# Causal attention on one Trainium2 core: even and odd query tiles on the two column halves of the array, weights summed on GpSimd, sums inverted through DRAM

## What is computed

```python
q = (x @ w_q) ...; k = (x @ w_k) ...              # 8 heads of 64
gates = sigmoid(x @ w_gate); sel = argmax(gates)  # 8 experts a head
gm = one_hot(sel) * gates
values = einsum('bhne,ehdk,bnd->bhnk', gm, value_experts, x)
sim = einsum('bhid,bhjd->bhij', q * SCALE, k)
sim = where(causal_mask, finfo.min, sim)
attn = softmax(sim, axis=-1)
out = einsum('bhij,bhjk->bhik', attn, values)
out = einsum('bhne,ehkd,bhnk->bhnd', gm, output_experts, out).sum(axis=1)
```

## Time and profile before

| | us |
|---|---|
| median of 3 runs | 974.07 |
| profiled execution, its own time | 970.34 |
| its span, first to last instruction | 968.6 |
| TensorE busy | 931.0 |
| VectorE busy | 680.5 |
| ScalarE busy | 389.7 |
| GpSimd busy | 239.3 |
| mean granted TensorE clock | 0.996 of full speed |

### The profile page before, as it was taken

One profiled execution on the slowest core, in us unless ns is written; L12 is line 12 of the kernel. 1 busy time (PEld: TensorE's weight loads), 2 busy tenths in 40 slices (PEclk: granted clock), 3 DMA queues, 4 the chain that ended last, 5 costly groups with the idle time before them and its releaser, 6 DMA issues.

```text
span 968.6 us, 14634 instructions
## 1 busy us (share of the span) xinstructions
PE 931.0 (96%) x5580; PEld 721.1 (74%) x5580; DVE 680.5 (70%) x1054; ACT 389.7 (40%) x678; POOL 239.3 (25%) x253
## 2 busy tenths in 40 slices
PE   6989899999999999999999998999999999999998
PEld 3568678887666655899966786888876656569998
DVE  4858566547557877898868666754674777879887
ACT  4635555030566766401034355720115655751000
POOL 6212322222533322146610032300041101411000
PEclk9999999999999999999999999999999999999999
DMA  7112000524245511255630000022220000023663
GB/s 258 50 37 96 1 1 8 170 91 131 66 154 194 198 43 44 65 176 175 190 115 1 1 1 1 1 94 87 86 82 7 23 22 1 25 75 101 194 181 124
DMA packets 33739, 81.56 MB, mean 84 GB/s; under 512 B 5847, under 2 KB 10551, under 8 KB 33671
## 3 DMA queue, kind: packets, MB, share of 16 engines
q1 hardware_dynamic: 32391, 76.44, 24.9%
q10 hardware_dynamic: 1280, 4.20, 1.6%
HBM read 61.26 MB, written 19.20 MB: 83 GB/s over the span
## 4 chain that ended last, share of the span: by engine, by line
PE 81%; DVE 11%; issue 3%; ACT 3%; DMA 1%; ACTq 0%; POOL 0%; SPq 0%; DVEq 0%; POOLq 0%
PE ps L1109 18%; PE ps L1436 10%; PE ps L1373 9%; PE ps L1442 5%; PE ps L1333 5%; PE ps L1288 5%; PE ps L1117 4%; PE ps L1349 4%; PE ps L1240 3%; DVE region L1001 3%; PE ps L1302 3%; PE ps L1409 3%; PE ps L1410 2%; PE ps L1255 2%; PE ps L1151 2%
## 5 line engine op out<-in xcount | busy, mean ns | idle before, releaser
L1373 PE MATMUL ps<-region 128*128 128x512 f32 (+3 forms) x384 | 161.4, 503 | 0.0
L980 DVE TENSOR_REDUCE region<-ps 128x1 f32<-128x512 f32 (+1 forms) x192 | 98.1, 550 | 63.9 <-PE ps L1352 63.8
L761 ACT ACTIVATE region<-ps 128x512 f32<-128x512 f32 x192 | 92.3, 487 | 122.6 <-PE ps L1412 110.8
L1025 DVE COPY_PREDICATED region<-region,ps 128x512 f32<-128x512 uint32 x112 | 82.0, 735 | 72.1 <-PE ps L1109 71.4
L1436 PE MATMUL ps<-expert_hi,kst 128*128 128x256 f32 x512 | 125.1, 283 | 3.0 <-DVE kst L1055 2.2
L1436 PE MATMUL ps<-expert_lo,kst 128*128 128x256 f32 x512 | 123.3, 279 | 0.0
L1109 PE MATMUL ps<-expert_hi,wide_hi 128*128 128x512 f32 x256 | 102.7, 401 | 0.0
L551 ACT ACTIVATE region<-ps 64x512 f32<-64x512 f32 (+4 forms) x148 | 82.1, 557 | 48.3 <-PE ps L1255 21.2
L1109 PE MATMUL ps<-expert_hi,wide_lo 128*128 128x512 f32 x256 | 100.1, 391 | 0.0
L1109 PE MATMUL ps<-expert_lo,wide_hi 128*128 128x512 f32 x256 | 99.8, 390 | 0.0
L1436 PEld LDWEIGHTS ps<-expert_hi,kst 128*128 128x128 f32 x512 | 96.3, 188 | 4.2 <-DVE kst L1055 2.6
(11 more groups left out here) (151 smaller groups left out, 1764.1 us busy)
## 6 DMA issues: line engine op xcount, KB each, us to landing
region<-hot_rows SPq DMA_DIRECT2D x128, 128.0 KB, 3.3
expert_hi<-halves_kept SPq DMA_DIRECT2D x24, 512.0 KB, 3.6
expert_lo<-halves_kept SPq DMA_DIRECT2D x24, 512.0 KB, 5.1
halves_kept<-expert_hi SPq DMA_DIRECT2D x16, 512.0 KB, 5.2
halves_kept<-expert_lo SPq DMA_DIRECT2D x16, 512.0 KB, 5.9
expert<-in_value_experts SPq DMA_DIRECT2D x8, 512.0 KB, 4.2
expert<-in_output_experts SPq DMA_DIRECT2D x8, 512.0 KB, 4.3
gb<-gate_rows ACTq DMA_DIRECT2D x16, 256.0 KB, 3.9
```

What stands on the lines that cost most here:

```text
L761: act.activation(PT[:, g % RING, lo:CH], ps[:, 4 + g % 2, 0:CH - lo], ACT.Exp).then_inc(sem["pt_ready"], 1)
L980: dve.tensor_reduce(mx[:, i, at_mx:at_mx + 1], ps[:, max_bank(h, m), 0:w], AX.X, ALU.max).then_inc(sem["s_max"], 1)
L1025: dve.copy_predicated(V3_heads[:, t], chosen.unsqueeze(3).broadcast_to([P, PAIRS3, 2, HD3]), ps[:, n % 4, :].rearrange("p (a i k) -> p a i ...
L1373: mm(ps[:, SUM_BANK[c], lo:CH], V3[:, j, h // 2, h % 2 * HD3:(h % 2 + 2) * HD3], PT[:, g % RING, lo:CH], start=(j == 0), stop=(j == TC * ( ...
```

## The change

- A block is now ordered by key tile, then chunk. The exps of one key tile for all its queries are kept whole, in places that stand free (`kept`: xT, the old PT space and the x of the other batch element, whose load moves behind the first attention).
- `weigh(h, j)` does one key tile: two products with 64 stationary columns (values only), the even query tiles into PSUM partitions 0 to 63 and the odd ones into 64 to 127 of one bank. It is called behind block 6 (tiles 0, 1), block 9 (2, 3) and block 1 of the next head (4 to 7).
- GpSimd adds the weights of key tiles 1 to 7 into those of tile 0 (`add_weights`), and `denominators(h)` sums them over the partitions with two products against ones, behind block 6 of the next head; for the last head behind output step 1.
- For the first three pairs the sums go to DRAM and come back as 128 rows of 16, VectorE inverts them and multiplies by the gates (`factors`), they go to DRAM again and are broadcast into `gb`, and one multiplication per part is left. The last pair is inverted in its full form.
- The second half of `qq` and `kx` are made by DMAs on ScalarE's queue instead of copies.
- `project` stands behind `scores` in its block; the places of rounding, of pieces and of the last normalisations move.

```diff
     G = H3 * E3
-    BLOCKS = [(c, j) for c in range(NC) for j in range(TC * (c + 1))]
+    BLOCKS = [(j, c) for j in range(TT) for c in range(j // TC, NC)]
     NB = len(BLOCKS)
+    LAST_BLOCK = [max(n for n, (x, _) in enumerate(BLOCKS) if x == j) for j in range(TT)]
...
+        den_cols = hg_all[:, BY_COLUMNS * KN:(BY_COLUMNS + 2) * KN].rearrange("p (i k) -> p i k", i=2)
+        sets = lambda v: v.rearrange("p (u s c) -> p u s c", s=2, c=P)
+
+        def total(h):
+
+            return xT[:, h % 2, :]
+
+            if j == 0:
+                return total(h)
+            home = PT_all if j in (1, 2, 5) else X[:, 1 - b].rearrange("p t d -> p (t d)")
+            return home[:, KEPT_AT[j]:KEPT_AT[j] + (TT - j) * P]
...
+        ROUND_AT = {(5, 4): 0, (5, 6): 1, (6, 4): 2, (6, 6): 3, (7, 9): 4, (7, 11): 5}
-        NORMALISED_AFTER = (0, 1, 4)
+        NORMALISED_AFTER = (1, 2, 4)
...
-        SUM_BANK = (3, 7)
+        SUM_BANK = (7, 3)
+        LATE_AT, SUMS_AT, EARLY_AT, MIDDLE_AT = 1, 6, 6, 9
+        OUT_AT, DEN_AT = 3, 8
...
-            sp.dma_start(X[:, 1, :, :], xv[1]).then_inc(x_next, 16)
...
+            def keep_den(b, h):
+
+                until(sp, "den_sb", b, den_copies(h))
+                sp.dma_start(den_rows[b, h].rearrange("(u s c) -> s u c", s=2, c=P),
+                             rden[0:P:HALF, h % 2 * CH:(h % 2 + 1) * CH].rearrange("s (u c) -> s u c", c=P)
+                             ).then_inc(den_kept, 16)
+            def turn_den(b, p):
+
+                n = b * BY_COLUMNS + p
+                sp.wait_ge(den_kept, 32 * (n + 1))
+                if n >= 2:
+                    sp.wait_ge(factors_kept, 16 * (n - 1))
+                sp.dma_start(den_cols[:, p % 2, :], columns_of(den_rows[b, 2 * p:2 * p + 2])).then_inc(den_in, 16)
+            def spread_factors(b, p):
+
+                n = b * BY_COLUMNS + p
+                until(sp, "factors_ready", b, p + 1)
+                sp.dma_start(columns_of(factor_rows[b, 2 * p:2 * p + 2]), den_cols[:, p % 2, :]
+                             ).then_inc(factors_kept, 16)
+                sp.wait_ge(factors_kept, 16 * (n + 1))
+                until(sp, "oT_ready", b, NC * p)
+                for i in range(2):
+                    sp.dma_start(gb[i * HALF:(i + 1) * HALF, :],
+                                 factor_rows[b, 2 * p + i:2 * p + i + 1, :].broadcast_to([HALF, S])
+                                 ).then_inc(gates_in, 16)
...
+                if b + 1 < B:
+                    until(sp, "av_used", b, H3 * TT)
+                    until(sp, "summed", b, H3 * (TT - 1))
+                    sp.dma_start(X[:, b + 1, :, :], xv[b + 1]).then_inc(x_next, 16)
...
+                def add_weights(h, j):
+
+                    done = h * (TT - 1) + j - 1
+                    if j == 1:
+                        until(pool, "av_used", b, h * TT + 1)
+                    until(pool, "pt_ready", b, h * NB + LAST_BLOCK[j] + 1)
+                    part = total(h)[:, j * P:]
+                    pool.tensor_tensor(part, part, kept(b, h, j), ALU.add).then_inc(sem["summed"], 1)
+                    until(pool, "summed", b, done + 1)
+                        if n in LAST_BLOCK[1:]:
+                            add_weights(h, LAST_BLOCK.index(n))
...
+                def queries_twice(h):
 
                     i, own, oth = h % 2, HALF * (h % 2), HALF * (1 - h % 2)
-                    if k == 0:
-                        until(act, "qk_sb", b, (h // 2 + 1) * 2 * NC)
-                        if h >= 2:
-                            until(act, "st_ps", b, (h - 1) * NB)
-                        copy(qq[i][own:own + HALF, :], raw[own:own + HALF, 0, :], "qq_ready")
-                    elif k == 1:
-                        copy(qq[i][oth:oth + HALF, :], raw[own:own + HALF, 0, :], "qq_ready")
-                    else:
-                        copy(kx[i][own:own + HALF, :], raw[own:own + HALF, 1, :], "kx_ready")
+                    until(act, "qq_ready", b, h + 1)
+                    act.dma_start(qq[i][oth:oth + HALF, :].bitcast(fp32), qq[i][own:own + HALF, :].bitcast(fp32)
+                                  ).then_inc(qq_in, 16)
+
+                def keys_twice(h):
+
+                    i, own = h % 2, HALF * (h % 2)
+                    until(act, "kst_ready", b, 2 * h + 1)
+                    act.dma_start(kx[i][own:own + HALF, :].bitcast(fp32), kst[i][own:own + HALF, :].bitcast(fp32)
+                                  ).then_inc(kx_in, 16)
 
...
                     act.wait_ge(rows_kept, 32 * (b + 1))
-                    until(act, "oT_ready", b, NC * p)
+                    until(act, "den_ps", b, H3 - 1)
+                    until(act, "oT_ready", b, NC * (p - 1) + 1)
...
+                def output_copy(h, s):
+
+                    own, r = HALF * (h % 2), slice(s * HALF, (s + 1) * HALF)
+                    until(act, "av_used", b, (h + 1) * TT)
+                    copy(sets(oT[own:own + HALF, h // 2, :])[:, :, s, :],
+                         ps[r, SUM_BANK[h % 2], :].rearrange("p (u c) -> p u c", c=P), "o_sb")
+
+                def den_copy(h):
+
+                    own, den = HALF * (h % 2), ps[:, SUM_BANK[h % 2], :]
+                    until(act, "den_ps", b, h + 1)
+                    if h < 2 * BY_COLUMNS:
+                        n = 2 * BY_COLUMNS * b + h - 1
+                        if n > 0:
+                            act.wait_ge(den_kept, 16 * n)
+                        copy(rden[:, h % 2 * CH:(h % 2 + 1) * CH], den, "den_sb")
+                    else:
+                        act.wait_ge(den_kept, 32 * BY_COLUMNS * (b + 1))
+                        for s in range(2):
+                            copy(sets(rden[own:own + HALF, :])[:, :, s, :],
+                                 den[s * HALF:(s + 1) * HALF].rearrange("p (u c) -> p u c", c=P), "den_sb")
...
+                        if j == 0 and h >= 2:
+                            until(act, "den_ps", b, h - 1)
+                        if j and h:
+                            until(act, "av_used", b, (h - 1) * TT + j + 1)
+                            until(act, "summed", b, (h - 1) * (TT - 1) + j)
+                        act.activation(kept(b, h, j)[:, q0 - j * P:q1 - j * P], ps[:, 4 + g % 2, 0:q1 - q0], ACT.Exp
+                        if h + 1 < H3 and n == 0:
+                            queries_high(h + 1)
+                        if h + 1 < H3 and n == 1:
+                            queries_twice(h + 1)
+                        if h + 1 < H3 and n == 2:
+                            keys_twice(h + 1)
+                        if h and n in (OUT_AT, OUT_AT + 1):
+                            output_copy(h - 1, n - OUT_AT)
+                        if h and n == DEN_AT:
+                            den_copy(h - 1)
+                        if (h, n) == (H3 - 1, MIDDLE_AT):
+                            spread_gates()
                         if (h, n) in ROUND_AT:
                             rounded(ROUND_AT[h, n])
...
+                def factors(p):
+
+                    n = b * BY_COLUMNS + p
+                    if p == 0:
+                        dve.wait_ge(gate_cols_in, 16 * BY_COLUMNS * (b + 1))
+                    dve.wait_ge(den_in, 16 * (n + 1))
+                    step(dve.reciprocal(den_cols[:, p % 2, :], den_cols[:, p % 2, :]))
+                    dve.tensor_tensor(den_cols[:, p % 2, :], den_cols[:, p % 2, :], gate_cols[:, p, :], ALU.mult
+                                      ).then_inc(sem["factors_ready"], 1)
+                    if p >= BY_COLUMNS:
+                        step(dve.tensor_tensor(rden[:, cs], rden[:, cs], factors_of(p)[:, cs], ALU.mult))
+                    until(dve, "o_sb", b, 2 * (2 * p + 2))
+                    dve.tensor_tensor(oT[:, p, cs], oT[:, p, cs], (gb if p < BY_COLUMNS else rden)[:, cs], ALU.mult
...
+                    _, c0, c1 = PARTS[k]
+                    until(dve, "den_sb", b, den_copies(H3 - 1))
+                    step(dve.reciprocal(rden[:, c0:c1], rden[:, c0:c1]))
...
+                    if h >= 4 and h % 2 == 0:
+                        factors(h // 2 - 2)
+                    if h >= 4 and h % 2 == 0:
+                        weighted(h - 4)
+                        weighted(h - 3)
+                factors(BY_COLUMNS - 1)
+                weighted(H3 - 4)
+                weighted(H3 - 3)
...
-                        until(pe, "qq_ready", b, 2 * h + 2)
+                        pe.wait_ge(qq_in, 16 * (b * H3 + h + 1))
...
+                def weigh(h, j):
-                    mm(ps[:, SUM_BANK[c], lo:CH], V3[:, j, h // 2, h % 2 * HD3:(h % 2 + 2) * HD3],
-                       PT[:, g % RING, lo:CH], start=(j == 0), stop=(j == TC * (c + 1) - 1)
-                       ).then_inc(sem["av_used"], 1)
+                        if j == 0:
+                            until(pe, "val_v", b, TT * (E3 - 1))
+                    if j == 0 and h >= 2:
+                        until(pe, "den_sb", b, den_copies(h - 2))
```

(34 more changed lines are left out.)

170 lines of the change are left out of this document (86 added, 84 removed).

## The result

The changed kernel takes 1031.1 us (median of 4 runs, 1028.8 to 1032.9) against 974.2 us: a ratio of 1.0586, with a 95% interval of 1.0557 to 1.0616. The profiled execution takes 1030.4 us with a span of 1028.6, 60.1 us more than the one of before. Forecast were 1024 us and slower with 0.84.

The account below looks back on a forecast made before the run. TensorE was taken as the bound (96% busy, 81% of the chain). Profiled 970.3 us plus 9.9 and 12.7 (heads), 22.4 (last head), 2.0 (DRAM), 3.4 (clock) made 1020.7, as a median 1024 us; range 988 to 1050.

Parts of the forecast that it names:

- the forecast's sign: Weighted sums on TensorE, one of the signs that would show the forecast right: busy for 60% of the earlier time.
- The transfer's latency and issue: Second query half by DMA: issued at 3.4 us, 3.6 or 4.0 to land; scores start at 7.0 instead of 4.08.
- The wait for the row of maxima: In heads without a projection, only score block 9 covers the reduction after the last score: 0.6 us of waiting.
- The clock in the heads: TensorE's waits of about 3 us in the heads: no clock loss counted, 24 us as the other end.
- rival (c): The clock also falls in the heads, 24 us more: 1048 us; chance 0.2.
- trip through DRAM: Heads 4 and 5's sums via DRAM: 1 us waiting per batch element, 2 in all; other end 8.
- Behind the last head: Head 7's denominators and division in the output loop: 11.2 us per batch element, 22.4 in all, plus 3.4 for clock.
- What TensorE saves: Paired column halves run together in the weighted sums: 2.6 us saved in a head, 41 in sixteen heads.
- (a): Faster: scores not late, so the heads give back 35 us while the end costs 22; 961 us; chance 0.11.
- (b): Heads lose as forecast, but the division behind the last head is covered or lands earlier: 999 us; chance 0.12.
- (d): The column halves do not overlap with real operand sizes, 4.3 us in 16 heads: 1093 us; chance 0.02.
- (e): GpSimd's additions at twice their time make the denominators hold TensorE, about 1.5 us a head: 1048 us; chance 0.07.

Follow-up runs that it names:

- experiment 1: The changed kernel with the queries' second half made by ScalarE's copy again instead of the DMA: 998.1 us, ratio 1.0272.
- experiment 4: The changed kernel without the last pair's reciprocals and their multiplication by the gates (heads 6 and 7 not normalised): 1013.6 us, ratio 1.0438.
- experiment 2: The changed kernel with unread filling products on TensorE, six before each head's wait for queries and thirty before the output steps' wait: 1023.4 us, ratio 1.0525.
- experiment 9: The changed kernel with GpSimd's additions in head 7 from key tile 4 on cut to one column: 1024.9 us, ratio 1.0537.
- experiment 3: The changed kernel without the odd query tiles' products for key tiles 1 to 6: 1035.4 us, ratio 1.065.
- experiment 8: On top of experiments 7, ScalarE copies the queries' own half before the first exp instead of behind it: 984.0 us, ratio 1.0110.
- experiments 7: On experiment 1 plus earlier last-head denominators: row of maxima behind the second weighted sums, pair weightings behind the key splitting: 988.6 us, ratio 1.0154.

## Why the forecast was right, and where it wasn't

**Slower, by the forecast mechanisms: right.** The first scores are late by a transfer into qq in all 14 heads, one wait of over 7 us stands in each batch element's output steps, the reciprocals of 256 columns are gone from the heads. Taking the transfer away gives back 33 us (experiment 1), the last division 17.5 (experiment 4). The weighted sums with their ones-products are busy for 93.7 us instead of 161.4, 58% where the forecast's sign was 60%.

**The transfer's latency and issue: mis-sized, too large in quiet heads, too small in loaded ones.** The sum took 3.6 and 4.0 us from the nearest transfer; measured are 2.9 (the median of 16) and up to 6.2. That one reads DRAM, this one moves within SBUF. The Trainium skill ("DMA: Bandwidth & Descriptors", Anatomy of one DMA) has 2.0 us fixed, for transfers from GpSimd's queue, while this one is ScalarE's; the estimate of 2.6 that the forecast set beside its own is nearer to the 2.9 than the row was. The issue was put behind the exp at 3.4 us, and it came at 2.5. So a quiet odd head (3 or 5) lost 0.4 us and not 1.9, which is what 5.45 instead of 7.0 us makes of the forecast's own formula (1.9 - 1.55 = 0.35). Head 4 of the first batch element lost 6.4. Head 0, for which the sum had 0.3, lost 1.6 and, in the second batch element, 3.9: its transfer took 4.5 us there, TensorE waited 3.19 us, and two periods at the lower clock followed.

**The wait for the row of maxima: nearly right.** 0.6 us were forecast in heads without a projection; it is 0.5 us in all 14, those with a projection too; in the program the projection's products stand behind the row of maxima.

**The clock in the heads: the step that failed.** The forecast took nothing for the waits in the heads, with 24 us as the other end and 0.2 for rival (c), because TensorE is fully busy before and after. The mean granted clock fell from 0.996 to 0.972: over the spans, 1028.6 x 0.028 less 968.6 x 0.004 is 24.9 us of full clock withheld. There are 15 more periods of 3.4 us at the lower level than in before, eleven in the heads and four behind the 7.3 us waits. In the heads they cost up to 11 x 1.7 = 19 us. What this looks like in the changed kernel, first around the wait of 3.19 us that ends at 764.16, then behind the one of 1.57 us that ends at 806.31:

```profile
763.10:769.90 6.80, 5.74 (x18) 4.47 (x19) 1.49 (x4) 0.94 (x2) 0.00 (x0) 0.50 0.11 19
...
807.40:810.80 3.40, 3.40 (x12) 2.52 (x11) 0.50 (x2) 1.09 (x3) 0.00 (x0) 0.51 0.01 2
```

Without this loss the heads would have grown by some 9 and 5 us, less than the 12.7 and 9.9 of the sum. By the sum the heads (with the trip through DRAM) and the time behind the last head had 24.6 and 25.8 us; measured are 32.1 and 27.9. Two errors of opposite sign met in the heads: the transfer was priced too high, the clock at nothing. That the total came within 7 us is partly luck.

**Behind the last head: right in sum.** 22.4 us of denominators and division and 3.4 for the clock are 25.8; the output steps grew by 14.2 + 13.7 = 27.9. The long wait is 7.28 (forecast 7.5), 1.47 and 1.85 follow (2.2 and 1.65), and the denominators take 1.03. The clock is at 1.2 GHz from within the wait until some 3.3 us behind it, as forecast, but the 1.7 us that the sum has for it each time were not a cost: with the full clock (experiment 2) step 3 comes no earlier. In its place stands that VectorE needed 5.9 us from the end of masking 2 to that of masking 3 (435.47 to 441.40) where the sum had 5.0; the masking at 435.38, beside GpSimd, took 2.30 instead of 1.22. The 0.75 us ahead of step 1 weren't foreseen; they are contention (experiment 9). So two terms of this part were off as well and nearly cancel.

**The trip through DRAM: right.** 1 us in each batch element was forecast. The weightings of heads 4 and 5 start only at 412.73, released by the spread factors, and the masking behind them is what step 0 waits for, 1.05 us; it makes head 7 15.6 us long instead of 14.4. The contention has a part in it: the two weightings take 4.67 us, where two undisturbed ones of the earlier trace rows take 1.4. In experiment 9 the first of them, at 414.95, began just before the additions and took 0.69, and that head 7 lasts 14.5 us: most of the microsecond is the contention's.

**What TensorE saves: right in kind.** The halves overlap (0.85 us a pair, and experiment 3). With the waits and most of the clock loss removed, a quiet odd head takes 16.3 us instead of 17.3 (experiment 8), 1 us; the 2.6 forecast for the products must partly be given back in the waits for the row of maxima and for the exps that experiments 7 and 8 show; this part wasn't isolated.

**The rivals.** (a) fell: the transfer was quicker than thought and the scores still late. (b) fell. (c) happened: the clock cost up to 19 us in the heads where the rival had 24, and the waits themselves cost less than the sum had. (d) fell (experiment 3). (e), GpSimd as the bound, happened only as contention: its 397.9 us stay beside TensorE, and experiment 9 shows 1 us per batch element at the start of the output steps. What it costs in mid-head wasn't isolated.

**Open.** By how much the loaded heads' transfers were late because of the weight pieces, and by how much because of the keys' transfer issued behind them, wasn't tried.
